# A GNN gather layer: the one-hot matrix of each chunk made alone by a one-input compare, in place of eight at a time by a two-input operation

## The reference

```python
xn = layernorm(x)
def hconv(h, W, b):
    t = h @ W
    m = segment_sum(t[src], dst) / max(count by dst, 1)
    return segment_sum(m[dst], src) / max(count by src, 1) + b
g = prelu(hconv(prelu(hconv(xn, W1, b1)), W2, b2) + xn)
x = x + g + linear_attention(xn)
x = x + mixture_of_8_experts(layernorm(x))      # the top 2 of 8 for each node
```

## Time and profile before

| what | value |
|---|---|
| runs before, median (lowest to highest) of 3 | 8259.9 us (8250.78 to 8261.66) |
| profiled execution: its span, first to last instruction | 8262.6 us |
| profiled execution: its own time | taken as its span, no other is given |
| mean granted TensorE clock | 0.726 of full |
| gather passes 0, 1, 2, 3 | 1281 to 3157, 3198 to 4553, 4640 to 5950, 5982 to 7277 us |
| one-hot operations (line 921) | 444, 545.0 us busy |
| chunk sums (line 916) | 3520, 1482.8 us busy |
| gather issues (line 492) | 3520, 3508.1 us busy |

### The profile page before, as it was taken

How to read it: one execution, slowest core, us unless ns; L and a number is a source line. 1 busy time by engine, 2 the same in 40 slices (tenths; PEclk the granted TensorE clock), 3 DMA queues, 4 the chain that set the end, 5 groups by cost and what they waited for, 6 DMA issues and landing times. The chain is left out here.

```text
span 8262.6 us, 93487 instructions
## 1 busy us (share of the span) xinstructions
PE 4799.4 (58%) x16274; PEld 2762.7 (33%) x16275; DVE 3919.4 (47%) x9146; ACT 1396.4 (17%) x4207; POOL 4241.7 (51%) x4243
## 2 busy tenths in 40 slices
PE   3111776666666664666666355555456555554896
PEld 2000333333333332434443233333232322334564
DVE  8411995455445444444444444444433333366323
ACT  2100553333333330000000000000000000000242
POOL 0467003444444445666666466666667666632342
PEclk6555997778777786777776667776666666666898
DMA  4000001222222224333333334444543333331114
GB/s 166 14 0 0 2 0 51 60 60 60 60 60 60 58 61 116 88 91 90 90 92 87 98 113 116 118 115 114 123 135 91 88 90 89 89 76 38 39 62 132
DMA packets 330989, 639.10 MB, mean 77 GB/s; under 512 B 81808, under 2 KB 201444, under 8 KB 330448
## 3 DMA queue, kind: packets, MB, share of 16 engines
q0 software_dynamic: 191808, 490.67, 22.1%
q1 hardware_dynamic: 131396, 140.16, 5.2%
q10 hardware_dynamic: 7756, 7.97, 0.3%
HBM read 551.49 MB, written 87.01 MB: 77 GB/s over the span
## 5 line engine op out<-in xcount | busy, mean ns | idle before, releaser
L492 POOL DMA_INDIRECT gbuf<-table,idxb x3520 | 3508.1, 997 | 2884.0 <-ACT idxb L616 1692.0
L1281 PE MATMUL PS<-gbuf,ohg 128*128 128x257 f32 x7040 | 2732.1, 511 | 1755.0 <-issue 1004.0
L916 DVE TENSOR_TENSOR acc<-acc,PS 128x257 f32 x3520 | 1482.8, 421 | 2506.0 <-remote 964.2
L1281 PEld LDWEIGHTS PS<-gbuf,ohg 128*128 128x128 f32 x7040 | 1520.2, 242 | 2883.1 <-issue 1688.3
L1249 PE MATMUL PS<-region 128*128 128x440 f16 x5120 | 1272.6, 383 | 1159.3 <-ACT region L607 774.6
L1249 PEld LDWEIGHTS PS<-region 128*128 128x128 f16 x5120 | 502.1, 104 | 1779.0 <-ACT region L607 926.6
L616 ACT COPY idxb<-idx 128x4 int32 (+1 forms) x884 | 167.7, 191 | 3323.2 <-PE PS L1281 1960.6
L839 DVE TENSOR_SCALAR region<-iota_c,acc 128x880 f16<-128x880 f16 x835 | 395.0, 473 | 703.3 <-remote 571.5
L921 DVE TENSOR_TENSOR ohg<-iota,dl 128x1024 f32<-128x1024 f16 x444 | 545.0, 1227 | 81.5 <-issue 55.1
L606 ACT ACTIVATE region<-region,acc 128x128 f16<-128x128 f16 x835 | 335.2, 401 | 1230.0 <-DVE region L840 983.5
L501 POOL DMA_INDIRECT scattered_d<-acc x384 | 369.8, 963 | 142.7 <-issue 129.1
(11 more groups left out here) (262 smaller groups left out, 3094.0 us busy)
## 6 DMA issues: line engine op xcount, KB each, us to landing
gbuf<-table,idxb POOLq DMA_INDIRECT x3520
table<-acc SPq DMA_DIRECT2D x21, 896.0 KB, 6.7
region<-xt_d SPq DMA_DIRECT2D x98, 128.0 KB
gbuf<-ye_d SPq DMA_DIRECT2D x12, 1024.0 KB, 7.9
xpad_d<-acc SPq DMA_DIRECT2D x1, 6272.0 KB, 20.0
xn_d<-acc SPq DMA_DIRECT2D x49, 128.0 KB, 1.7
xt_d<-acc SPq DMA_DIRECT2D x49, 128.0 KB, 1.7
table<-acc SPq DMA_DIRECT2D x49, 128.0 KB, 1.7
```

The lines of the kernel that those rows point to most:

```text
L492: gp.indirect_dma_start(gbuf[:, k, 0:F], None, tables[p], bass.IndirectOffsetOnAxis(idxb[:, k:k + 1], 0)).then_inc(s_g[k], 16)
L916: TT(a, a, PS[:, 4 + k % AB, 0:FC], ALU.add).then_inc(s_acc[p], 1)
L1281: MM(PS[:, 4 + k % AB, 0:FC], ohg[:, k, :], gbuf[:, k, :], start=True, stop=True).then_inc(s_mm[p], 1)
```

## The change

Each chunk's one-hot is made alone. Operation k compares `iota_1` with one number per partition, a single column of `dl`, where before one operation compared two tensors for eight chunks. It stands on VectorE's queue directly before sum k and makes the slot of chunk k + 8; the first eight are made ahead of the loop. It waits for the product that used the slot last. The semaphore `s_ohg` counts chunks and no longer sets of eight: TensorE waits for it at each chunk, and the next pass waits for 880 + 8.

```diff
+    OH = 8
...
-            def one_hots(p, i, h):
-
-                dve.wait_ge(s_mm[p], i * U + (8 * h + 8))
-                TT(ohg[:, 8 * h:8 * h + 8, :], iota_1[:, :].unsqueeze(1).broadcast_to([P, 8, P]),
-                   dl[p % 2][:, ds(i * U + 8 * h, 8)].unsqueeze(2).broadcast_to([P, 8, P]), ALU.is_equal).then_inc(s_ohg[p], 1)
+            def one_hot(p, i, k):
+
+                dve.wait_ge(s_mm[p], i * U + (k + 1))
+                TS(ohg[:, k % U, :], iota_1[:, :], dl[p % 2][:, ds(i * U + k, 1)], None, ALU.is_equal).then_inc(s_ohg[p], 1)
 
             def acc_pass(p, start, end, body=None, links=0):
                 if start == 0:
                     if p:
-                        dve.wait_ge(s_ohg[p - 1], 2 * TURNS + 1)
-                    one_hots(p, 0, 0)
+                        dve.wait_ge(s_ohg[p - 1], NC + OH)
+                    for k in range(OH):
+                        one_hot(p, 0, k)
...
                     for k in range(U):
                         if body is not None:
                             body(i, k)
-                        if k == 1:
-                            one_hots(p, i, 1)
-                        if k == 9:
-                            one_hots(p, i + 1, 0)
+                        one_hot(p, i, k + OH)
                         add_chunk(p, i, k, block_of)
...
                     for k in range(U):
-                        if k % 8 == 0:
-                            pe.wait_ge(s_ohg[p], i * 2 + (k // 8 + 1))
+                        pe.wait_ge(s_ohg[p], i * U + (k + 1))
                         pe.wait_ge(s_g[k], (i + (p * TURNS + 1)) * 16)
                         pe.wait_ge(s_acc[p], i * U + (k + 1))
                         MM(PS[:, 4 + k % AB, 0:FC], ohg[:, k, :], gbuf[:, k, :], start=True, stop=True).then_inc(s_mm[p], 1)
```

## The result

The changed kernel took 8769.95 us (median of 4 runs, 8739.74 to 8783.61) against 8257.97 us (8250.78 to 8261.66), 1.0614 times, 95% interval 1.0593 to 1.0634. That is +512 us where +173 was forecast: the sign was right, the size outside the range. "The first chip" is the one of this comparison. Ratios are always to the kernel before on the same chip.

The account below looks back on a forecast made before the run. GpSimd's gather issue was taken to pace passes 1 to 3, stopped at times by VectorE's slow queue. Collisions −130, queue entries +233 and pass 0 +70 gave +173 us on 8262.6: 8435 us, range 8350 to 8600.

Parts of the forecast that it names:

- Part 1 and 2: Passes 1 to 3: long gather collisions go, −158 us; collisions of the new one-input compares cost 28 us; net −130 us.
- Part 3: VectorE's queue, passes 1 to 3: entries a chunk rise from 4.4 to 7, GpSimd stalls more often, +233 us.
- the ring: The 16 gather buffers GpSimd fills and TensorE's products free; forecast full after 10 us, not 13, stopping GpSimd.
- standstill: GpSimd's stop between runs of gathers when the buffers are full, 4.18 us in pass 3; forecast to keep its length.
- the crawl: While GpSimd issues gathers without a break, after about ten microseconds, VectorE's queue passes one instruction per 0.70 us.
- double if the crawl lengthens too: Upper bound on the +233 us of added GpSimd stalls in passes 1 to 3; the lower bound was 0.
- Part 4: Pass 0: added VectorE queue entries lengthen each turn by 1.3 us, +70 us over 52 turns; bounds −20 and +120 us.
- Part 5: TensorE's wait for the one-hot at each chunk never holds; its extra queue entry is hidden, costing nothing.
- C: VectorE's queue never leaves the crawl in passes 1 to 3; if standstills double, 8780 us; chance 0.08 together with D.
- A: Gathers freed, the crawl independent of VectorE's entries: about 8135 us, or 8195 with half the gain lost; chance 0.28.
- B: Collision gain and queue-entry loss cancel, stall factor near 1.2: 8245 to 8275 us; chance 0.07.
- D: New compare still holds the port, all 158 us of collisions stay, queue costs added: 8565 us; chance 0.08 together with C.

Follow-up runs that it names:

- the new version: Kernel before with two-chunk one-hots, no wait of their own, places copied once a turn to a fixed tile: 0.9817 (chip 15), 0.9811 (chip 14).

## Why the prediction was wrong in size, and where it was right

**Part 1 and 2, the collisions: right.** −130 us net for passes 1 to 3. On the first chip the issue time fell by 148.5 us there, on chip 15 the passes fell by 130, and the issue time in them by as much (2640.7 to 2510.7 us). Gathers are at 948 to 951 ns in these passes and at 958 in pass 0, where 946 to 960 was named. The new compare takes 281 ns at the median (249 was the nearest row). Of the rule of the Trainium skill (SBUF — State Buffer, the two separate sides), that two SBUF inputs take the lock, the runs show this: the two-input operation left gathers at a mean of 997 ns when it was 1220 ns long, at 961 ns with two chunks and 419 ns (chip 6), and at 956 ns single and 285 ns long, against 952 ns with the one-input compare of 281 ns. Between these forms the length of the operation made far more difference than the number of its inputs. That the new compare may still take the lock fits too: some issues are still longer than 946 ns, up to 1156. The formula of the Trainium skill (VectorE: DVE Perf Modes, errata), (N + 151)/0.96, gives an estimated 424 ns for 256 columns, and the trace has 419.

**Part 3, the queue entries: right in kind, wrong in size.** The step that failed is "the ring is full after 10 us … with the same standstill behind it. Stalls per gather rise by 20/13". It let standstills become more frequent and kept their length. Taken off the idle times in the same way as for the kernel before (264 us of gaps, and 70 and 25 us), the stalls of passes 1 to 3 are 460, 364 and 353 us, 1177 together, against 527: a factor of 2.2 where 1.3, 1.54 and 1.54 were taken. By the count of standstills above, in passes 2 and 3 runs became shorter, as said: 12.1 and 13.8 gathers for one standstill where 13 was forecast, from 16.0 and 22.6. But each standstill became 1.5 times as long. In pass 1 runs did not become shorter at all, 15.7 gathers after 13.5, and the standstill went from 3.3 to 8.2 us; that pass also grew most, by 192 us. A chunk in the crawl took 5.6 to 5.7 us, not 4.9. For the length the cycle above offers a reason: at 5.6 us a sum fewer sums pass in the standstill's first part, and those that are owed must pass before the next buffers are free. That reason is not tested, and why pass 1 is hit hardest stays open. With +650 us in place of +233 the sum would have been −130 + 650 + 70 = +590, and with pass 0 as measured +558, against 519. The bound "double if the crawl lengthens too" was the right place to look; it was kept out of the range.

**Part 4, pass 0:** +38 us measured, +70 forecast, within its bounds, but the way there is not shown. The forecast read 16.5 us of a turn as 24 steps of 0.70. The trace has no such step there: between 2094.6 and 2111.15 us no register or wait entry of VectorE took over 57 ns, they pass in bunches, and the time lies between the bunches. In all of pass 0 the kernel before has 11 entries of over 0.5 us. That the size is near is in part luck.

**Part 5, TensorE's extra wait:** nothing to be seen: 8797 us with the wait thinned, 8778 us in the two-input variant that keeps it.

**Rivals.** C named the time, 8780 us, but not the way: in the cycle shown the queue does get out of the crawl (0.6 us a sum from 6516.13 on). A (faster, 0.28) is refuted on the first chip by the +512 us, and on chip 11 time falls with the entries. Its outcome is how the other chips are, where nothing crawls: −144 us in the passes on chip 15, and 0.98 on 6 and 15. Its clause that half the gain may go to a ring that fills sooner fits chip 11: 8430 us with 0.8 entries more at 207 us and 158 us less would be 8438 us, and 8517 was measured, 79 us of the 158 not there. That is worked out and not shown by a run. B (a factor near 1.2) is out by the 2.2, D by the issue times.

**What could not have been read from one trace.** The forecast took 0.70 us a queue entry for a property of the kernel; it is one of where or when it runs. The changed kernel met the crawl in the first comparison and its variants on chip 11; on chips 6 and 15 it met none, nor did its relative, the new version, on chip 14. Without saying which kind of chip, the sign of this change is open. Whether the crawl belongs to a chip or to a time wasn't settled: no chip was seen in both conditions.

## What to carry to other kernels

Before costing a change by a slow row, look at its minimum, median and maximum: a register instruction of 1/40/1398 ns is held by something that the profile does not name, and a second chip may not have it at all. Where queues crawl, count entries (registers, waits, operations) and not busy time alone, and expect a standstill to lengthen as well as to come sooner; where they do not, a short VectorE operation a chunk in place of a long one for eight frees the software gathers, and here it was worth 2% on chips 6 and 15. Time a change on more than one chip before it is kept or dropped.

## What the runs showed of the hardware that was not expected

- The crawl isn't VectorE's alone. SyncE's register move takes 682 ns at the median in the kernel before on the first chip and 29 ns on chip 15, and GpSimd's register instructions of line 490 reach 710 ns there and never pass 32 ns here. Those of TensorE (line 1275 of the changed kernel) keep to 32 to 36 ns on both, and those of ScalarE (line 606) to 46 to 60. Nor is every entry of VectorE's queue held: the sort's register instructions of line 840, which run up to the end of pass 0, never passed 65 ns in the kernel before:

```profile
L387 SPq MOVE region<-xt_d x49: 4/682/712, 4639.2 to 5791.1; - x49
L490 POOLq ALU_OP  x3300: 4/32/710, 1282.9 to 7265.0; - x195
L606 ACTq FUSED_REGOPS  x1280: 46/46/60, 291.0 to 3093.2; - x183
L840 DVEq FUSED_REGOPS  x1280: 57/57/65, 290.2 to 3092.6; - x183
```

```profile
L387 SPq MOVE region<-xt_d x49: 29/29/38, 3373.9 to 4392.0; - x49
L490 POOLq ALU_OP  x3300: 32/32/32, 952.9 to 5712.9; - x195
```

- The first chip and chip 15 are some 1550 us apart in this kernel (8262.6 against 6709.6 us of span): 1281 against 952 us up to pass 0, and 5836 against 4602 us in the four passes. How much of that is the crawl is not shown. What makes a chip crawl stays open; bytes moved and packets are the same on both (639.1 MB, 330,989 packets, on the pages of the kernel before). The gathers' transfers do not lag either: with 48 packets to a gather, taken in order, the last is done at the median 2.4 us after the issue's start in pass 3 on the first chip, and 2.3 us on chip 15.
- TensorE's granted clock moved with it, and the other way than the time: in pass 3 of the kernel before it is 0.65 of full on the first chip and 0.56 on chip 15, at 741 and 983 us of busy time, and that pass is still 148 us shorter.
